# Two layers of a gated mixture-of-experts kernel: the second layer's shared weights are loaded and split earlier, and its shared blocks follow their tile by two steps instead of three

## The chip, the cores and the metric

The kernel runs on one core of one Trainium2 chip. The metric is the device time of one execution in microseconds. Three runs of the kernel before took 1601.77, 1603.18 and 1605.84 us, median 1603.18.

## The reference

The input x has 4 x 512 tokens of 512 numbers. Two layers are added to it one after the other. Each layer first mixes over the tokens (a decaying sum forward and backward along the tokens, over a side input, divided by the same sum of weights, times a sigmoid of x), and then applies a mixture of experts. Layer 0 has an RMS norm, 8 experts of inner size 256 of which each token takes 2, and one shared expert. Layer 1 has 32 experts of inner size 352 of which each token takes 6, and two shared ones, which are run as two halves.

```python
# layer 1, cut to what matters
top_w, top_i = lax.top_k(softmax(xf @ gate_w.T), 6)
routed = sum over the 6 of  top_w * ((silu(x @ w1[e]) * (x @ w3[e])) @ w2[e])
shared = silu(xf @ sw1) * (xf @ sw3) @ sw2
x = x + routed + shared
```

## The kernel before

The tokens are 16 tiles of 128. The work is a sequence of blocks of 128 tokens. Block 0 to 15 are layer 0's shared expert, 16 to 54 its routed blocks (39), 55 to 86 layer 1's shared blocks (32, two for each tile, one for each half of the shared weights), and 87 to 214 its routed blocks (128). For each block TensorE multiplies by gate and up (`gu_pe`, line 1714), ScalarE takes a tanh and VectorE finishes H (`gu`), TensorE transposes H (`h_turn`, 1752), ScalarE and VectorE split it into a high and a low half in float16, TensorE multiplies by the down weights (`down`, 1778), and ScalarE (line 1222) or VectorE (line 1594) takes the result out.

Weights are products of three float16 matmuls, so each weight is needed as a high and a low half. `pieces` (line 80) cuts them into pieces of 1024 or 1088 columns. A piece is loaded by SyncE (`w_load`, 918) into one of two staging buffers ST, whose order is RING, or, for the pieces in AHEAD, straight into a part of Whi or Wlo that is not yet used. ScalarE then makes the high half (`w_hi`, 1148: one pass where VectorE makes the low half, two passes where POOL does), and VectorE (`w_lo`, 1542) or POOL (`w_lo`, 971) the low half. A ring load waits until the piece two before it in the ring has its low half. Pieces 0 to 26 are layer 0's, 27 to 34 layer 1's shared weights (27 to 30 for even shared blocks, 31 to 34 for odd ones), 35 and up layer 1's experts. In `pieces` 27, 29, 31 and 33 belong to VectorE and 28, 30, 32 and 34 to POOL, and 35 to 50 to POOL. `spare` (731) gives the block after whose `down` the place of a piece may be written: for 27 to 50 that is block 54, the last routed block of layer 0.

The order of all work is written out by hand in `stages` (115), a generator. Every engine walks it and takes what is its own, so the order in it is the program order of each engine. After layer 0's shared blocks a loop over j runs from 0 to 41 (line 392). Step j has `gu_pe` of block 16+j, a half of a unit of the second layer's scan in two of three steps, `h_turn`, `gu`, `h_low`, and `down` of block 13+j. A unit of the scan has 128 channels of one batch: the first half is two forward scans, a scaling on ScalarE (1073, 1075) and two backward scans (1285 to 1299), and the second half is sums and a reciprocal (1306 to 1321), with two products on POOL (955, 963). Then TensorE turns the result (`k_turn`) and ScalarE writes it to RT (1092). At j from 37 to 40 SyncE issues `y_load`, the first of which waits for the last RT. For the routed blocks POOL gathers rows (`gather`, 978) into three buffers XG and SyncE transposes them by DMA (`x_turn`, 894) into four buffers XSp.

Then come `pick` 0 and 1 (POOL gathers the routed results of layer 0), four pieces by `weights`, and `x_sum` 0 and `f_tanh` of the first tile. `x_sum` (1335) adds what was picked into the tile. A loop over s from 0 to 17 (line 429) follows. Step s has, for tile s: the turn of tile s-1 on TensorE (`f_turn`, 1630), `gate` of tile s on VectorE (1324), `f_hi` on ScalarE (1116) and `f_lo` on VectorE (1353), both in the one buffer XG[2], `row` and `x_turn` on SyncE. `f_hi` waits for the transposition of the tile before. Then come two slots h, each with one shared block b = 2(s-3)+h: `gu_pe` of b, `h_turn` of b-1, `gu` of b, `down` of b-2. In between stand the logit of the tile before, `x_sum` and `f_tanh` of the next, and after every fourth tile the routing: `r_top`, `r_red`, then `r_pos`, `r_wts`, `r_slot`. `hot` makes two 0/1 matrices on VectorE, `hot_pe` multiplies them; there are 24 of each, and from the third on `hot` waits until the `hot_pe` two before is done. The step ends with two pieces of weights (one from s=4 on). After the loop come hot 18 to 23, the last blocks, hot_pe 18 to 23 and the gathers for block 87. `hot_pe` 18 stands behind `gu_pe` of block 86.

Of the kernel before, what the change touches and what calls it, by code (L numbers as in the profile page):

```python
# [92 lines left out]

AHEAD = (17, 18, 19, 20)
RING = [k for k in range(len(PIECES)) if k not in AHEAD]


# [15 lines left out]
def stages():  # L115
# [24 lines left out]
    def weights(n, upto):  # L140
        for _ in range(n):
            yield from loads(2, upto)
            yield from splits(1)
            yield from loads(2, upto)
# [247 lines left out]
    for j in range(NB0 + 3):  # L392
        n = R0 + j
        if n + 3 < S1:
            yield "gather", n + 3
        if n + 2 < S1:
            yield "x_turn", n + 2
        if n < S1:
            yield "gu_pe", n
        yield from turn_made()  # L400
        if j * 27 // 39 != (j - 1) * 27 // 39 or j >= 39:
            yield from next_half()
        if n - 1 < S1:
            yield "h_turn", n - 1
        if n < S1:
            yield "gu", n
        yield from after_half()
        if n - 2 < S1:
            yield "h_low", n - 2
        if 1 <= j:  # L410
            yield "down", n - 3
        if 37 <= j < 41:
            yield "y_load", j - 37
    while half[0] < 64:
        yield from next_half()
        yield from after_half()
    yield from turn_made()
    for i in range(2):
        yield "pick", i
    yield from weights(4, 51)  # L420
    yield "x_sum", 0
    yield "f_tanh", NT

    def shared(b, what):

        if 0 <= b < 32:
            yield what, S1 + b

    for s in range(18):
# [11 lines left out]
        if s < 8:  # L441
            yield "k_back", s + 8
        for h in (0, 1):
            b = 2 * (s - 3) + h
            slot = 2 * s + h
            yield from shared(b, "gu_pe")
            yield from shared(b - 1, "h_turn")
            yield from shared(b, "gu")
# [97 lines left out]
def build(nc, xtok, fT, cst, svec, cond, rout, gatew, W0, W1, Y1):  # L546
    with ExitStack() as ctx:
# [5 lines left out]
        def sem(name):  # L553
            return ctx.enter_context(nc.semaphore(name))
# [104 lines left out]
        d_pick = [sem(f"d_pick{i}") for i in range(2)]  # L659
        d_first = sem("d_first")  # L660
        d_w = [sem(f"d_w{i}") for i in range(2)]
        d_ahead = sem("d_ahead")
        d_g = [sem(f"d_g{i}") for i in range(3)]
        d_t = [sem(f"d_t{i}") for i in range(4)]
        d_row = [sem(f"d_row{i}") for i in range(6)]
# [55 lines left out]
        def staged(k):  # L721

            l, e, c0, cw, at, who = PIECES[k]
            if k in AHEAD:
                m = AHEAD.index(k)
                to = 18432 + 3072 * (m // 2)
                return (Whi, Wlo)[m % 2][:, to:to + 2 * cw].bitcast(F32), d_ahead, 16 * (m + 1)
            m = RING.index(k)
            return ST[m % 2][:, 0:cw], d_w[m % 2], 16 * (m // 2 + 1)

        def spare(k):

            if k < 27:
                return None
            m = (k - 27) // 4
            if m < SLOTS1:
                return S1 - 1
            return R1 - 1 if m - SLOTS1 < 2 else R1 + 4 * (m - SLOTS1 - 2) + 3
# [96 lines left out]
        def _(eng):  # L835
# [82 lines left out]
            def w_load(k):  # L918
                l, e, c0, cw, at, who = PIECES[k]
                if k not in AHEAD and k >= 2:  # L920
                    eng.wait_ge(*low(RING[RING.index(k) - 2]))
                at, there, count = staged(k)
                S.dma_start(at, WD[l][e][:, c0:c0 + cw]).then_inc(there, 16)

# [121 lines left out]
        def _(eng):  # L1046
# [101 lines left out]
            def w_hi_(k):  # L1148
# [3 lines left out]
                eng.wait_ge(there, count)  # L1152
                if k == 21:

                    for j in AHEAD[-2:]:
                        eng.wait_ge(*low(j))
                if spare(k) is not None:
                    eng.wait_ge(b_down, spare(k) + 1)
# [73 lines left out]
        def _(eng):  # L1232
# [230 lines left out]
            def hots(h):  # L1463

                A16, B16 = AB[h % 2][:, 0], AB[h % 2][:, 1]
                if h >= 2:
                    eng.wait_ge(r_tab, 1 + h - 1)
                else:
                    eng.wait_ge(b_down, S1)
                n0 = 4 * h % 24  # L1470
                V.tensor_tensor(A16, bc(iota16[:, :].unsqueeze(1), [P, 4, P]),
                                bc(qa[:, n0:n0 + 4].unsqueeze(2), [P, 4, P]), ALU.is_equal)
# [393 lines left out]
```

## Time and profile before

| | us |
|---|---|
| median of 3 runs | 1603.18 |
| the profiled execution | 1601.73 |
| its span, first to last instruction | 1599.6 |
| TensorE (PE) busy in the span | 1342.6 (84%) |
| VectorE (DVE) busy | 1006.1 (63%) |
| ScalarE (ACT) busy | 742.2 (46%) |
| GpSimd (POOL) busy | 604.6 (38%) |

The shares are means over very different stages: layer 0 until some 513 us, the shared stage of layer 1 until some 807 us, then its routed blocks. Times in the rows are microseconds from the start of the span. An entry in brackets is the time that the engine was idle before the instruction, and what released it.

### The profile page before, as it was taken

Reading aid. Unit: us, or ns where it says so; the run is one execution under the profiler, and the core shown is the slowest. Engines: PE = TensorE matmul, PEld = TensorE weight load, DVE = VectorE, ACT = ScalarE, POOL = GpSimd, SP = SyncE. Lnnn points to the kernel's source line nnn. Section 1 sums busy time; section 2 is a strip of 40 time slices with the busy share of each in tenths; the row PEclk is TensorE's granted clock in tenths of the full one; section 3 lists DMA queues with packets and bytes.
Section 4 is the critical chain, followed back from the end, with each engine's and each line's share of the span. In section 5 each row is a group of like instructions: output and inputs, shape, how many; then the busy total and the mean of one; then the engine's idle time right before and its main releaser. Section 6 shows DMA issues by size and latency. Waiting matters only on the chain.

```text
span 1599.6 us, 23683 instructions
## 1 busy us (share of the span) xinstructions
PE 1342.6 (84%) x8220; PEld 811.3 (51%) x8220; DVE 1006.1 (63%) x1748; ACT 742.2 (46%) x1262; POOL 604.6 (38%) x466
## 2 busy tenths in 40 slices
PE   0146666699997289889899999999999999999998
PEld 0023342244443156556565666666666666666664
DVE  8999978979896468888735444444444444444222
ACT  4466664545454543333146454454444445444332
POOL 2344432544431443231033443444444444444443
PEclk9987766899999599999999999999999999999999
DMA  3557644689985896563048988889998988988664
GB/s 101 174 174 187 156 112 92 151 182 195 206 177 159 227 205 145 141 146 83 25 137 233 203 199 212 196 207 199 207 208 195 206 203 204 200 206 184 109 115 74
DMA packets 225234, 269.38 MB, mean 168 GB/s; under 512 B 149664, under 2 KB 149792, under 8 KB 224992
## 3 DMA queue, kind: packets, MB, share of 16 engines
q1 hardware_dynamic: 188464, 175.84, 42.6%
q0 software_dynamic: 36656, 92.03, 29.2%
q8 instruction: 70, 1.15, 0.3%
q14 instruction: 44, 0.36, 0.1%
HBM read 167.87 MB, written 70.32 MB: 149 GB/s over the span
## 4 chain that ended last, share of the span: by engine, by line
PE 60%; DVE 26%; issue 5%; DMA 4%; ACT 3%; POOL 1%; SPq 0%; POOLq 0%; ACTq 0%; DVEq 0%
PE psG L1749 33%; PE psO L1798 19%; DVE wkFD L1314 5%; PE psH L1766 3%; DMA ST<-W 2%; DVE wkFN L1289 2%; DVE wkFD L1296 2%; PE psX L1710 2%; DVE wkFD L1285 2%; DMA XSp<-XG 2%; DVE wkFN L1321 1%; DVE wkFD L1306 1%; DVE H L1574 1%; DVE Wlo L1555 1%; DVE wkFN L1299 1%
## 5 line engine op out<-in xcount | busy, mean ns | idle before, releaser
L1749 PE MATMUL psG<-Whi,XSp 128*128 128x352 f16 (+2 forms) x3000 | 671.8, 329 | 12.1 <-issue 10.8
L1749 PEld LDWEIGHTS psG<-Whi,XSp 128*128 128x128 f16 x3000 | 295.7, 100 | 212.5 <-issue 38.4
L1798 PE MATMUL psO<-Whi,HS 128*128 128x512 f16 (+1 forms) x1180 | 394.5, 387 | 0.0
L1749 PE MATMUL psG<-Wlo,XSp 128*128 128x352 f16 (+2 forms) x1500 | 389.2, 329 | 0.0
L1021 POOL DMA_INDIRECT out<-OB,posb x128 | 202.7, 1583 | 416.1 <-ACT OB L1222 407.5
L1555 DVE SCALAR_TENSOR_TENSOR Wlo<-ST,Whi 128x1088 f16<-128x1088 f32 (+1 forms) x118 | 152.3, 1291 | 235.4 <-ACT Whi L1168 231.4
L1574 DVE SCALAR_TENSOR_TENSOR H<-H,psG 128x352 f32<-128x352 f32 (+1 forms) x215 | 105.5, 491 | 242.2 <-ACT H L1187 221.4
L1798 PE MATMUL psO<-Wlo,HS 128*128 128x512 f16 (+1 forms) x590 | 228.4, 387 | 0.0
L1187 ACT ACTIVATE H<-psG 128x352 f32<-128x352 f32 (+1 forms) x215 | 95.2, 443 | 229.7 <-PE psG L1749 222.5
L1749 PEld LDWEIGHTS psG<-Wlo,XSp 128*128 128x128 f16 x1500 | 149.1, 99 | 93.4 <-issue 8.3
L1798 PEld LDWEIGHTS psO<-Whi,HS 128*128 128x128 f16 x1180 | 117.6, 100 | 120.4 <-issue 9.8
L1222 ACT ACTIVATE OB<-psO,WSL 128x512 f32<-128x512 f32 x128 | 88.1, 688 | 173.7 <-PE psO L1798 173.7
L1003 POOL DMA_INDIRECT XG<-xrows,posb x128 | 129.5, 1012 | 90.9 <-DVE posb L1486 42.4
L1168 ACT ACTIVATE Whi<-ST 128x1088 f16<-128x1088 f32 (+1 forms) x118 | 129.7, 1100 | 28.1 <-DMA ST<-W 28.1
L975 POOL TENSOR_TENSOR Wlo<-ST,Whi 128x1088 f16<-128x1088 f32 (+1 forms) x37 | 82.0, 2218 | 154.6 <-ACT Whi L1172 154.5
L1576 DVE SCALAR_TENSOR_TENSOR H<-H,psG 128x352 f32<-128x352 f32 (+1 forms) x215 | 106.4, 495 | 7.4
L1200 ACT CAST HS<-psH 128x384 f16<-128x384 f32 x160 | 75.7, 473 | 71.9 <-PE psH L1766 71.9
L963 POOL TENSOR_TENSOR wkFN<-wkFN,wkEU 128x512 f32<-128x512 f32 x32 | 40.5, 1267 | 180.6 <-DVE wkEK L1276 169.5
L1314 DVE RECIPROCAL wkFD<-wkFD 128x512 f32<-128x512 f32 x32 | 107.1, 3346 | 0.0
L1620 PE MATMUL psX<-C,wkFN 128*128 128x128 f32 x64 | 16.7, 412 | 101.9 <-DVE wkFN L1321 101.9
L1584 DVE TENSOR_TENSOR HS<-psH,HS 128x384 f16<-128x384 f32 x160 | 88.1, 551 | 16.2 <-ACT HS L1200 16.2
L1766 PE MATMUL psH<-C,H 128*128 128x128 f32 x480 | 80.5, 277 | 19.3 <-DVE H L1576 19.3
(216 smaller groups left out, 1536.9 us busy)
## 6 DMA issues: line engine op xcount, KB each, us to landing
ST<-W SPq DMA_DIRECT2D x136, 544.0 KB
ST<-W SPq DMA_DIRECT2D x23, 512.0 KB
slots<-OB SPq DMA_DIRECT2D x39, 256.0 KB
wkK<-fT SPq DMA_DIRECT2D x32, 256.0 KB
xrows<-XG SPq DMA_DIRECT2D x20, 256.0 KB, 4.4
y0rows<-x SPq DMA_DIRECT2D x8, 512.0 KB, 5.5
y0rows<-OB POOLq DMA_DIRECT2D x16, 256.0 KB, 4.3
out<-OB SPq DMA_DIRECT2D x16, 256.0 KB
```

Of the source, the lines that this page charges most:

```text
L1003: G.indirect_dma_start(out=XG[g % 3][:, 0:w], out_offset=None, in_=X[l][:, :], in_offset=bass.IndirectOffsetOnAxis(ap=idx[l][:, j:j + 1], ...
L1021: G.indirect_dma_start(out=Y1[:, :], out_offset=bass.IndirectOffsetOnAxis(ap=idx[1][:, j:j + 1], axis=0), in_=OB[o % 4][:, :], in_offset=N ...
L1168: op = A.activation(st if who == "pool" else hi, st, ACT.Copy, scale=WS)
L1187: A.activation(H32[a][:, 0:F], psG[a][0][:, 0:F], ACT.Tanh, scale=0.5 * UN).then_inc(b_tanh, 1)
L1222: A.activation(OB[o % 4][:, :], psO[bank(o)][:, :], ACT.Copy, scale=scale).then_inc(b_outa, 1)
L1314: V.reciprocal(FD[n % 2][:, :], FD[n % 2][:, :]).then_inc(k_rec, 1)
L1555: op = V.scalar_tensor_tensor(out=Wlo[:, at:at + cw], in0=st, scalar=WS, in1=Whi[:, at:at + cw], op0=ALU.mult, op1=ALU.subtract)
L1574: V.scalar_tensor_tensor(out=H, in0=H, scalar=1.0, in1=g, op0=ALU.add, op1=ALU.mult).then_inc(b_sil, 1)
L1576: V.scalar_tensor_tensor(out=H, in0=H, scalar=(-0.5, 0.5)[l] * XS * UN * UN, in1=u, op0=ALU.mult, op1=ALU.mult).then_inc(b_h, 1)
L1749: op = M.matmul(o, hx[:, x, q * P:q * P + P], w(half_, off + c, nn), start=first, stop=last)
L1766: op = M.transpose(bank_[:, q * P:q * P + P], H32[a][:, q * P:q * P + P], ident)
L1798: op = M.matmul(psO[bank(o)][:, :], hs(n)[:, x, q * P:q * P + P], columns[n](half_, off0 + q * 512, 512), start=(q == 0 and x == 0 and hal ...
```

## The change

AHEAD gets pieces 32 and 33, which are loaded into the place of layer 0's shared weights once all its shared blocks are done. Loads and splits of layer 1's shared weights are put into the loop over j, and the four pieces that stood before `x_sum` 0 are taken out. As the counters of `stages` work out, the loads are 27 and 28 at j=1, 32 at j=2, 33 at j=3, 29 and 30 at j=22, and 31 and 34 at j=37; the splits are 27 at j=20, 28 at j=21, 29 at j=35, 30 at j=36 and 31 at j=39. Step s=0 then splits 32 and 33, s=1 34 and 35, and so on, and the last pieces of the loop, 50, at s=14. `spare` lets 27 and 28 be written after block 31 (expert 0 has at most 16 blocks) and 29 to 31 after block 47. Two more waits guard the places of 32 and 33 before piece 47 and before `hot` 0 and 1. In the loop over s the shared block of slot 2s+h is now slot - 4, up to block 27 (of 0 to 31); steps 16 and 17 have one block each, 28 and 29, in their second slot.

```diff
-AHEAD = (17, 18, 19, 20)
+AHEAD = (17, 18, 19, 20, 32, 33)
...
         if 37 <= j < 41:
             yield "y_load", j - 37
+        if j in (1, 22, 23, 37):
+            yield from loads(2, 51)
+        if j in (2, 3):
+            yield "w_load", 30 + j
+        if j in (20, 21, 35, 36, 39):
+            yield from splits(1)
...
     for i in range(2):
         yield "pick", i
-    yield from weights(4, 51)
     yield "x_sum", 0
     yield "f_tanh", NT
...
         for h in (0, 1):
-            b = 2 * (s - 3) + h
             slot = 2 * s + h
+            b = slot - 4 if slot < 32 else {33: 28, 35: 29}.get(slot, -9)
...
-        d_ahead = sem("d_ahead")
+        d_ahead = [sem(f"d_ahead{i}") for i in range(6)]
...
             m = (k - 27) // 4
+            if k < 32:
+
+                return R0 + 15 if k < 29 else R0 + 31
...
+                if k in AHEAD and l == 1:
+
+                    eng.wait_ge(b_down, R0)
                 at, there, count = staged(k)
...
                 if k == 21:
 
-                    for j in AHEAD[-2:]:
+                    for j in AHEAD[2:4]:
+                        eng.wait_ge(*low(j))
+                if k == 27 + 4 * 5:
+                    for j in AHEAD[4:]:
                         eng.wait_ge(*low(j))
...
                     eng.wait_ge(b_down, S1)
+
+                    for j in AHEAD[4:]:
+                        eng.wait_ge(*low(j))
```

## Rows read from the trace of the kernel before

**Rows 1.** Windows: start:end, length, busy (instructions) by engine, TensorE clock, DMA share, GB/s.
```profile
core 0: us, PE busy (x) PEld busy (x) DVE busy (x) ACT busy (x) POOL busy (x), PEclk, DMA share, GB/s
340.00:360.00 20.00, 19.01 (x97) 9.46 (x95) 16.77 (x21) 11.16 (x26) 7.29 (x6) 1.00 1.04 237
...
550.00:560.00 10.00, 6.68 (x26) 4.67 (x27) 2.90 (x5) 4.25 (x6) 4.55 (x4) 0.50 1.17 256
...
662.55:724.09 61.54, 55.50 (x375) 36.14 (x375) 50.01 (x111) 21.79 (x37) 18.15 (x12) 0.97 0.57 141
...
752.57:788.10 35.53, 35.53 (x251) 22.97 (x249) 26.59 (x74) 5.21 (x13) 2.25 (x1) 1.00 0.07 25
```
**Rows 2.** Timeline of VectorE, 417 to 425 us: start, duration, instruction.
```profile
418.00 0.68 DVE L1306 SCALAR_TENSOR_TENSOR wkFD<-wkEU,wkFD 128x512 f32<-128x512 f32 x1
...
423.12 0.69 DVE L1321 SCALAR_TENSOR_TENSOR wkFN<-wkFD,wkFN 128x512 f32<-128x512 f32 x1
...
424.51 1.22 DVE L1285 TENSOR_TENSOR_SCAN wkFD<-dec,wkEK 128x512 f32<-128x512 f32 x1
```
**Rows 3.** Timelines of VectorE and ScalarE, 493 to 500 us.
```profile
494.25 0.42 DVE L1574 SCALAR_TENSOR_TENSOR H<-H,psG 128x256 f32<-128x256 f32 x1 [1.23 <-ACT H L1187]
...
495.04 1.22 DVE L1285 TENSOR_TENSOR_SCAN wkFD<-dec,wkEK 128x512 f32<-128x512 f32 x1
...
497.29 1.25 DVE L1296 TENSOR_TENSOR_SCAN wkFD<-dec,wkFD 128x511 f32<-128x511 f32 x1
...
494.96 0.60 ACT L1222 ACTIVATE OB<-psO 128x512 f32<-128x512 f32 x1 [0.47 <-PE psO L1798]
```
**Rows 4.** Timelines of SyncE's queue and of ScalarE, 504 to 524 us.
```profile
507.34 0.32 SPq L886 DMA_DIRECT2D wkK<-y0rows  x1
...
513.92 0.98 SPq L923 DMA_DIRECT2D ST<-W  x2
...
510.71 0.38 ACT L1205 ACTIVATE HS<-psH 128x256 f16<-128x256 f32 x1
...
512.93 0.60 ACT L1222 ACTIVATE OB<-psO 128x512 f32<-128x512 f32 x1 [0.70 <-PE psO L1798]
519.50 1.11 ACT L1168 ACTIVATE Whi<-ST 128x1088 f16<-128x1088 f32 x1 [5.97 <-DMA ST<-W]
```
**Rows 5.** Timelines of POOL, VectorE and TensorE, 505 to 560 us.
```profile
517.98 0.97 POOL L1035 DMA_INDIRECT wkFD<-slots,sl  x1 [14.76 <-DMA slots<-OB]
...
528.34 0.75 DVE L1341 SCALAR_TENSOR_TENSOR wkK<-wkFD,wk,wkK 128x512 f32<-128x512 f32 x1
...
531.87 2.30 DVE L1332 SCALAR_TENSOR_TENSOR XG<-XG,RT 128x512 f32<-128x512 f32 x1 [1.99 <-ACT XG L1108]
...
539.91 0.69 DVE L1332 SCALAR_TENSOR_TENSOR XG<-XG,RT 128x512 f32<-128x512 f32 x1
...
556.11 0.80 PE L1749 MATMUL psG<-Whi,XSp 128*128 128x352 f16 x2
```
**Rows 6.** The page's costliest groups: the splits of weights (busy, mean ns, idle before).
```profile
L1555 DVE SCALAR_TENSOR_TENSOR Wlo<-ST,Whi 128x1088 f16<-128x1088 f32 (+1 forms) x118 | 152.3, 1291 | 235.4 <-ACT Whi L1168 231.4
...
L1168 ACT ACTIVATE Whi<-ST 128x1088 f16<-128x1088 f32 (+1 forms) x118 | 129.7, 1100 | 28.1 <-DMA ST<-W 28.1
L975 POOL TENSOR_TENSOR Wlo<-ST,Whi 128x1088 f16<-128x1088 f32 (+1 forms) x37 | 82.0, 2218 | 154.6 <-ACT Whi L1172 154.5
```
**Rows 7.** Timeline of ScalarE, 417.5 to 424 us.
```profile
417.92 0.60 ACT L1222 ACTIVATE OB<-psO 128x512 f32<-128x512 f32 x1 [0.47 <-PE psO L1798]
```
**Rows 8.** Timelines of VectorE and POOL, 306 to 311 us.
```profile
307.33 3.08 DVE L1289 TENSOR_TENSOR_SCAN wkFN<-dec,wkEKV 128x512 f32<-128x512 f32 x1
...
306.71 2.62 POOL L975 TENSOR_TENSOR Wlo<-ST,Whi 128x1024 f16<-128x1024 f32 x1 [1.49 <-ACT Whi L1172]
```
**Rows 9.** Timelines of TensorE and VectorE, 752 to 792 us.
```profile
752.57 0.60 PE L1640 MATMUL psX<-C,XR 128*128 128x128 f32 x4
...
768.27 0.19 DVE L1384 MAX8 mx<-lg 128x8 f32<-128x32 f32 x1
...
788.10 0.69 DVE L1471 TENSOR_TENSOR Whi<-iota,qa 128x512 f16<-128x512 f16 x1 [1.44 <-PE psO L1685]
```

More of the change, by code:

```diff
@@ L726, in staged @@
                 to = 18432 + 3072 * (m // 2)
-                return (Whi, Wlo)[m % 2][:, to:to + 2 * cw].bitcast(F32), d_ahead, 16 * (m + 1)
+                return (Whi, Wlo)[m % 2][:, to:to + 2 * cw].bitcast(F32), d_ahead[m], 16
             m = RING.index(k)
```

## The prediction

> **What bounds the kernel now.** I read the windows by stage first, then the chain of waits, then the timelines of the engines where the change acts. While the first layer's routed blocks run, TensorE and VectorE are both nearly full, and the sixteen DMA engines are full in places: 19.0 and 16.8 of 20 us, DMA share 1.04 at 340 to 360 us [rows 1]. The reader should see there that this is no stage with room to spare. One unit of the scan (two halves on VectorE, with three blocks on TensorE) takes about 14.1 us: from 424.51 to 495.04 us five units pass [rows 2, 3]. VectorE waits in it for one loop (its H, the transposition, ScalarE's tanh), 1.23 us [rows 3], and for little else, so I read this stage as VectorE-bound: what VectorE loses there is not made up. In the second layer's shared stage four tiles take 61.5 us [rows 1], TensorE busy for 55.5 and VectorE for 50.0 of them. The shifting of blocks changes neither total, so I keep that cycle as it is. Between the stages TensorE does nothing useful from 512.9, when the last routed block's result is read [rows 4], to 556.11 us, when the first shared block starts [rows 5]. At the end of the shared stage TensorE is busy for all 35.5 us of 752.57 to 788.10 [rows 1].
>
> **The splits beside the routed blocks.** Five pieces (27 to 31) are loaded and split there, and 32 to 34 are loaded. A piece costs ScalarE 1.10 us, or two such passes if POOL makes the low half, and VectorE 1.29 us, or POOL 2.22 [rows 6]. Each engine takes them in program order, and what counts is who stands behind.
> Piece 27 (block j=20): its high half follows the scaling of `down` at 417.92 us on ScalarE [rows 7], so it runs from 418.5 to 419.6, and VectorE, which began its next half at 418.00, has to wait for it and then spends 1.29: 420.9. Cost 2.9 us on VectorE [rows 2, 6].
> Piece 28 (j=21) is POOL's. ScalarE's two passes for it end near 425.7, so its low half would start just as VectorE comes to k_out (423.12, shifted by 2.9, is 426.0) [rows 2]. When POOL subtracts, a VectorE operation with two inputs in SBUF waits: the scan at 307.33 took 3.08 us where one of the same size takes 1.22, and ended 1.1 after POOL did [rows 3, 8]. So k_out is pushed by about 1.8 us. Bounds: 0 (VectorE first) and 2.2.
> The Trainium skill, page SBUF — State Buffer, section on the shared port pair, says the same as a rule: whichever of the two starts first holds the pair for the whole instruction and the other fully blocks. By that rule piece 28 costs nothing if k_out comes a moment before POOL, and piece 30 costs the same; the sum would be 1.8 lower. The rows show the unlucky order, so I keep 1.8.
> Piece 29 (j=35) is VectorE's and falls into the idle 1.23 us before 494.25 [rows 3]: 0.1.
> Piece 30 (j=36): ScalarE finishes `down` at 495.56 and then makes two passes to 497.8, so its scaling of the forward scan comes late; the backward scan, at 497.29 before, would start at 498.5 [rows 3], meets POOL's subtraction and ends at about 501.3 instead of 498.5. Cost 2.8; bounds 1.2 (no meeting) and 3.
> Piece 31 (j=39): its load is issued behind the first y_load, which SyncE can issue only at 507.34, when the last RT is written [rows 4]. The first ring load of before was issued at 513.92 and its split started at 519.50 [rows 4], 5.6 later, so this one, issued after a store at about 507.7, is there at about 513.1. ScalarE waits for it and then takes 1.1, and the last block's low half, at 510.71 before, and its `down` stand behind. The last routed result then comes at 516.0 to 516.6 instead of 512.93. Cost 3.1; bounds 1 (the load lands in 4 us) and 5. The cover that looks plentiful, ScalarE's idle time, is gone here because ScalarE is made to wait for a DMA.
> Sum: 2.9 + 1.8 + 0.1 + 2.8 + 3.1 = +10.7 us at the end of the first layer.
> **The DMAs.** Eight loads of 544 KB are issued there, about 2.3 us of all DMA engines each at the 237 GB/s of 340 to 360 us [rows 1], four of them between 320 and 337 us, SyncE also waiting for all first-layer shared blocks before piece 32. Gather and transposition follow each other through three buffers, so late landings can stop TensorE; VectorE has some lead over them in two of three blocks. I take +1; bounds 0 and +7.
>
> **Between the layers.** The last `down` to the gate of the first tile: before, the result was read from 512.93, pick started at 517.98, x_sum at 528.34 (VectorE had two low halves to make), and the gate, blocked by a POOL subtraction for 1.6 us, ended at 531.87 + 2.30 = 534.17 [rows 4, 5]: 20.6 us after 513.5. After: nothing is loaded at the same time, so I put pick 3.1 after the result (before 4.4), its two issues and their landing at 5.8, then x_sum 1.5, tanh 0.6, gate 0.7: 11.8 us. Gain 8.8, with bounds 7 and 9.5. Then some is given back. Tile 1's gate ended at 540.60 [rows 5], 6.4 after tile 0's. Now pieces 32 (POOL) and 33 (VectorE) stand ahead of it: x_sum and both halves of tile 0 2.8, tanh 0.6, ScalarE 3.3, then a VectorE low half that waits for POOL's, 2.4, gate 0.7: 9.85. Loss 3.4. The next step holds two blocks at the low clock (clock 0.50 still at 550 to 560 us in the first blocks of before [rows 1]), and I put the first block about 1.7 us behind the turn of tile 1 and the turn of tile 2 at 15.0 us after the gate of tile 1. Before, the turn of tile 2 stood 14.6 after it, just ahead of the block at 556.11 [rows 5]: +0.4, and one step more +0.3. Net: -8.8 + 3.4 + 0.7 = -4.7. What is late next is again the tile chain: gate, high half, low half, transposition, one after the other in one buffer; starting the blocks a step earlier does not shorten it.
>
> **The end of the shared stage.** Two blocks are already done when the last tile is turned (752.57 [rows 9]), so steps 16 and 17 hold one each. Four steps hold eight blocks in 55.5 us of TensorE time [rows 1], some 6.2 each without the turns and logits. If TensorE bounded all of it, that were -12. But the last routing sum starts at 768.27, behind the logit and one block's `down` and hot matrices on VectorE [rows 9], and TensorE now reaches hot_pe 15 and 17 before VectorE has made them: it waits about 2.3 us twice. I get the routing sum 3.6 us earlier, r_pos, then no longer behind a block, 5.4 earlier, and hot 20, which waits for hot_pe 18 behind block 86 at 788.10 [rows 9], 5.5 earlier. After that all is as before. -5.5, bounds -3.5 and -7.5.
>
> **Sum.** +10.7 + 1 - 4.7 - 5.5 = +1.5 us on the profiled execution's 1601.7 (its span 1599.6 and 2.1 around it), which lies 1.5 below the median of the three runs, 1603.2. For the median that makes 1604.7; forecast 1604.5, no change that can be measured: a measurement of this kernel tells some 0.3% (4.8 us) from no change.
>
> **Rivals.** *The splits are hidden* (0.26). VectorE's delays are made up because TensorE, busy for 19.0 of 20 us [rows 1], takes its turn as the bound, and the load of piece 31 lands early; the layer end moves by 3 us, not 11. For it: VectorE is idle for 3.2 of 20 us, ScalarE for about nine [rows 1]. Against it: five units in a row average 14.1 us, and the 1.23 us of waiting is a fixed round trip, not TensorE being late. Time 1604.5 - 7.5 = 1597.
> *TensorE bounds everything* (0.04): the earlier start comes through, hardly anything is given back, about -15: 1589.
> *The loads starve the ring* (0.26), on the other side: four loads before 337 us and two at 428 us delay the gathers and with them the transpositions; in a stage at DMA share 1.04 the backlog of 9 us is worked off slowly, and each block that lands late holds VectorE's gate/up step. It decides as soon as a transposition lands over 2 us later than now. Price +7: 1611.5.
> *The change does not do what it says*: if `b_down` or the ring's counts held the early loads back, the splits would wait on ScalarE in the middle of the blocks. The counts work out (ring loads 27 and 28 need only pieces 25 and 26), so I leave it inside the starved case.
>
> **Numbers.** The forecast's own case has 0.44 and reaches from 1599 to 1609. A small part of the hidden and of the starved case also ends within 0.3%. The whole range goes to 1594 (the hidden case with the tail's better bound) and 1612 (the starved case). Left out are the TensorE case and the far ends, 0.15 or so. Faster 0.27, same 0.49, slower 0.24.
>
> **What would show it.** On the timeline of VectorE the unit with j=20 to 22 is longer by 4 to 5 us and that with j=36 by about 3; ScalarE shows a wait for a DMA before the last split of the first layer; the last routed result comes about 11 us later, at 524. The first x_sum follows it by 9 to 10 us, and the first shared block starts near 549, still at the low clock. Turn of tile 15 is about 7 us later than 752.6, the first routed block of the second layer about 1 later than 807. If the last routed result comes before 518, the first sum is wrong and the kernel is faster; if TensorE shows waits of over 2 us for XSp between 330 and 450 us, the starved case holds. If hot_pe 15 and 17 show no wait, the end gains more than I say.

## The result and the profile after

The changed kernel took 1609.6 us (median of 20 runs), the kernel before 1604.3 us (20 runs beside it). The ratio is 1.0033, with a 95% interval from 1.0018 to 1.0048: slower by about 5.3 us, a small difference that the interval just tells from no change. The forecast was 1604.5 us, no change; the time is inside its whole range (1594 to 1612), and just above the 1609 up to which its own case reaches. The profiled execution took 1609.4 us with a span of 1607.5, 7.9 us more than the span of the one before.

The page of the changed kernel, its head:

```profile
span 1607.5 us, 23686 instructions
...
PE 1346.7 (84%) x8220; PEld 809.3 (50%) x8220; DVE 1007.3 (63%) x1748; ACT 741.5 (46%) x1262; POOL 603.0 (38%) x466
```

No total says anything: the work is the same, moved. Windows of the changed kernel, columns as in [rows 1], the last two being the four steady tiles and the end of the shared stage:

```profile
440.00:450.00 10.00, 7.75 (x32) 3.75 (x31) 5.94 (x7) 2.99 (x7) 2.69 (x3) 0.83 0.94 214
...
674.70:736.29 61.59, 55.61 (x374) 36.15 (x374) 49.93 (x111) 21.79 (x37) 18.15 (x12) 0.97 0.61 140
764.90:793.08 28.18, 24.33 (x179) 15.63 (x177) 21.29 (x66) 3.43 (x8) 0.00 (x0) 1.00 0.07 22
```

The steady tiles are what they were (61.54 before). The end is 7.35 us shorter than the 35.53 of before, and TensorE is no longer busy all through it. In the window at 440 us, in which TensorE now idles for more than 2 us and part of the time has the low clock, lies one of the two large things that the forecast had put too low.

Since both kernels run the same instructions, every one can be paired with itself. The table is made so, from the start times of six of them: the first scan of units 25 and 31, ScalarE's read of the last routed result, the turns of tiles 5 and 15, and VectorE's first gate/up operation of block 87. The column before is in us, the others are the difference to it; one profiled execution each. The kernels e1 to e12 are told below.

| stage | before | changed | e1 | e2 | e3 | e4 | e6 | e7 | e9b | e10b | e11b | e12 |
|---|---|---|---|---|---|---|---|---|---|---|---|---|
| A: scan units 25 to 31 | 84.5 | +8.2 | +5.1 | +8.1 | +6.2 | +2.4 | +2.4 | +0.9 | +0.4 | +0.1 | +0.4 | 0.0 |
| B: to last routed result | 17.9 | +5.6 | +5.0 | +2.8 | +5.1 | -0.1 | -0.2 | -0.5 | -0.3 | 0.0 | -1.6 | -0.6 |
| C: to turn of tile 5 | 87.9 | -1.3 | -3.8 | -2.0 | -5.2 | +10.2 | -3.9 | -14.2 | -14.4 | -11.4 | -7.7 | -4.2 |
| D: to turn of tile 15 | 151.7 | +0.3 | +0.3 | +0.4 | +0.4 | -0.1 | +0.2 | 0.0 | +0.4 | +4.5 | +0.3 | +0.1 |
| E: to block 87 | 59.1 | -7.0 | -7.0 | -7.0 | +0.1 | -5.6 | -5.6 | 0.0 | +3.4 | 0.0 | -7.0 | -7.0 |
| A to E | 401.1 | +5.8 | -0.4 | +2.4 | +6.6 | +6.8 | -7.1 | -13.9 | -10.5 | -6.8 | -15.6 | -11.7 |

Behind E, where the code is the same, the profiled executions differ by up to 3 us from the one before (the changed kernel: +2.5). Ahead of A only the first four early loads are new. The twelve kernels that have them there, e5 and e8 included, reach A by -0.5 to +5.2 us later, 2.8 on average (the changed kernel: -0.5), and e4, which has not, 0.4 earlier. Within a stage two executions of the same code differ too: A of e4 is 2.4 longer than A of the kernel before, and A of e6 2.0 longer than A of e11b. So the table attributes, differences of some 2 us in it are not to be trusted singly, and the medians judge.

Stage A in the changed kernel. VectorE at the splits of pieces 27 and 28:

```profile
417.48 0.42 DVE L1594 SCALAR_TENSOR_TENSOR H<-H,psG 128x256 f32<-128x256 f32 x1
419.37 1.29 DVE L1573 SCALAR_TENSOR_TENSOR Wlo<-ST,Whi 128x1088 f16<-128x1088 f32 x1 [1.47 <-ACT Whi L1183]
420.57 0.68 DVE L1321 SCALAR_TENSOR_TENSOR wkFD<-wkEU,wkFD 128x512 f32<-128x512 f32 x1
...
425.69 2.47 DVE L1336 SCALAR_TENSOR_TENSOR wkFN<-wkFD,wkFN 128x512 f32<-128x512 f32 x1
```

The half that began at 418.00 in [rows 2] begins at 420.57: the wait of 1.47 for the high half and 1.29 of work, 2.8 us against the run's own offset of -0.2 there. Then k_out takes 2.47 instead of 0.69, 1.8 us, because POOL's subtraction had begun before it:

```profile
425.37 2.24 POOL L987 TENSOR_TENSOR Wlo<-ST,Whi 128x1088 f16<-128x1088 f32 x1 [0.37 <-ACT Whi L1187]
```

And then SyncE's queue:

```profile
434.78 0.93 SPq L935 DMA_DIRECT2D ST<-W  x2
435.80 1.23 SPq L916 DMA_TRANSPOSE XSp<-XG  x1
...
437.75 3.39 SPq L916 DMA_TRANSPOSE XSp<-XG  x1
```

and TensorE, for the block that waits for it:

```profile
442.87 0.39 PE L1767 MATMUL psG<-Whi,XSp 128*128 x1 [2.25 <-DMA XSp<-XG]
...
444.71 0.63 PE L1767 MATMUL psG<-Wlo,XSp 128*128 x1
445.14 1.06 PE L1767 MATMUL psG<-Whi,XSp 128*128 x2
```

The loads of pieces 29 and 30 go out together at 434.78. The transposition behind them takes 3.39 us to issue (1.30 at its place before) and lands so late that TensorE waits 2.25 us; after that its matmuls take 0.63 instead of 0.38 (clock 0.83 over the window above), and the scan's turn and both engines behind it stand 3.95 us later.

Stage B: VectorE at pieces 29 and 30.

```profile
500.68 1.28 DVE L1573 SCALAR_TENSOR_TENSOR Wlo<-ST,Whi 128x1088 f16<-128x1088 f32 x1
502.00 0.42 DVE L1592 SCALAR_TENSOR_TENSOR H<-H,psG 128x256 f32<-128x256 f32 x1
...
506.08 2.75 DVE L1311 TENSOR_TENSOR_SCAN wkFD<-dec,wkFD 128x511 f32<-128x511 f32 x1 [0.96 <-ACT wkFD L1085]
```

SyncE's queue at piece 31:

```profile
518.08 0.32 SPq L895 DMA_DIRECT2D wkK<-y0rows  x1
518.44 0.91 SPq L935 DMA_DIRECT2D ST<-W  x2
```

and ScalarE there, to the last routed result:

```profile
523.16 1.11 ACT L1183 ACTIVATE Whi<-ST 128x1088 f16<-128x1088 f32 x1 [2.62 <-DMA ST<-W]
...
526.24 0.60 ACT L1237 ACTIVATE OB<-psO 128x512 f32<-128x512 f32 x1 [1.21 <-PE psO L1816]
```

Piece 29 costs nothing: the gate/up operation behind it comes 7.75 us later than in [rows 3], as all around it. Piece 30 costs 2.5 (0.96 of waiting, and a scan of 2.75 instead of 1.25). Piece 31 costs 3.0: its load stands behind the first y_load, ScalarE waits 2.62 us for it, and the last result comes at 526.24.

Stage C, VectorE: the first sum, the gate of tile 0, the low half of piece 33 and the gate of tile 1.

```profile
535.89 0.75 DVE L1356 SCALAR_TENSOR_TENSOR wkK<-wkFD,wk,wkK 128x512 f32<-128x512 f32 x1 [10.29 <-DMA wkFN<-slots,sl]
...
538.12 0.69 DVE L1347 SCALAR_TENSOR_TENSOR XG<-XG,RT 128x512 f32<-128x512 f32 x1 [0.69 <-ACT XG L1120]
...
545.49 2.43 DVE L1573 SCALAR_TENSOR_TENSOR Wlo<-Wlo,Whi 128x1088 f16<-128x1088 f32 x1 [3.84 <-ACT Whi L1183]
547.84 0.68 DVE L1347 SCALAR_TENSOR_TENSOR XG<-XG,RT 128x512 f32<-128x512 f32 x1
```

The sum is 9.65 us behind the last result (15.41 before), the gate of tile 0 ends 12.6 behind it (21.2 before), and the gate of tile 1 comes 9.7 behind that.

### The profile page after: what moved, and what is told of

The parts are those of the page before. It is cut to its first block, busy times and chain, and to the rows that moved or that the text cites. A ratio compares the mean times of both kernels' runs of the same rounds, so it can differ in the third digit from the quotient of the medians.

```text
span 1607.5 us, 23686 instructions
## 1 busy us (share of the span) xinstructions
PE 1346.7 (84%) x8220; PEld 809.3 (50%) x8220; DVE 1007.3 (63%) x1748; ACT 741.5 (46%) x1262; POOL 603.0 (38%) x466
## 4 chain that ended last, share of the span: by engine, by line
PE 36%; DVE 26%; issue 16%; DMA 9%; POOL 7%; ACT 4%; POOLq 0%; SPq 0%; ACTq 0%; DVEq 0%
PE psG L1767 19%; PE psO L1816 12%; DVE wkFD L1329 5%; POOL out L1033 4%; DMA out<-OB,posb 4%; POOL XG L1015 3%; DMA ST<-W 3%; DVE wkFN L1304 2%; DVE wkFD L1311 2%; PE psH L1784 2%; DVE wkFD L1300 2%; DVE wkFN L1336 1%; DVE wkFD L1321 1%; DVE H L1592 1%; PE psX L1728 1%
## 5 line engine op out<-in xcount | busy, mean ns | idle before, releaser
L1602 DVE TENSOR_TENSOR HS<-psH,HS 128x384 f16<-128x384 f32 x160 | 88.0, 550 | 15.2 <-ACT HS L1215 15.2
```

## The experiments

Three questions were open: what the early splits and loads cost and why, whether the shift of the shared blocks is a gain, and whether places exist at which the same work costs nothing.

**e1: the two loads apart.**

```diff
-        if j in (1, 22, 23, 37):
+        if j in (1, 37):
             yield from loads(2, 51)
+        if j in (24, 28):
+            yield from loads(1, 51)
```

> The loads of pieces 29 and 30 are issued one by one, at j=24 and j=28, instead of together at j=22; all splits stay where the change puts them. In the changed kernel TensorE waits 2.25 us for XSp at 442.87 us and then runs a few us at the low clock, 4.0 us in all. Theory A (the two loads, 1.1 MB, stand ahead of a transposition on the DMA engines): the wait is gone, the scan unit that starts at 453.11 before is again 3.8 us late, not 7.8, and the last routed result of the first layer comes at 522.3 instead of 526.24 us. Theory B (POOL's low half of piece 28 holds back two gathers by 5 us, and those are what comes late): the wait stays, last routed result at 525.5 or later. Time about 1605.5 by A, 1609.5 by B.

One run: 1602.58 us. In the window in which the changed kernel has 7.75 us of TensorE work at clock 0.83:

```profile
440.00:450.00 10.00, 10.00 (x53) 5.06 (x51) 9.86 (x11) 5.33 (x12) 4.43 (x4) 1.00 1.05 206
```

Unit 27 takes 14.05 us instead of 18.01; theory A. POOL's low half of piece 28 and the gathers behind it are unchanged, so they are not the cause. e2 and e5, which keep the pair of loads, have the wait again (2.21 and 2.00 us) and a unit 27 of 18.0 and 17.6 us. e3 keeps it too and waits 2.29 us, but has no low clock there: its unit 27 takes 16.4. So some 2.3 of the 3.95 us are the wait and 1.6 the clock. A single load is no guarantee either: in this run TensorE waits 1.38 us for XSp at 453.88, which costs nothing, and in e8, also with single loads, 3.08 us at 455.66. The last routed result came at 523.97 and not at the expected 522.3, because this run was 2.3 us behind already at unit 26, 1.5 of it from ahead of the stage. The rest of the 7 us is not shown to come from the loads: stage C is 2.5 us shorter too, told below, and behind block 87 this run had 2.1 less.

**e2: the load of piece 31 ahead of y_load.** The four lines of the loads at j in (1, 22, 23, 37) and of y_load change places.

> The loads of j (31 and 34 at j=37) stand ahead of y_load instead of behind it; nothing else is moved. Theory A (ScalarE waits 2.6 us for a load that is issued only at 518.4 us, behind a y_load that waits for the last RT): the load is issued near 508 us, ScalarE's wait for it is gone, the last routed result comes 3.0 us earlier, at 523.2 instead of 526.24 us, and the time is about 3 us shorter, 1606.5. Theory B (the last down is late for another reason, TensorE's low clock or the chain of the last scan unit): under 1 us earlier, 525.3 or later, time unchanged.

One run: 1606.87 us. SyncE's queue and then ScalarE, at the same place as above:

```profile
510.18 0.93 SPq L935 DMA_DIRECT2D ST<-W  x2
519.91 0.33 SPq L895 DMA_DIRECT2D wkK<-y0rows  x1
```

```profile
521.82 0.60 ACT L1237 ACTIVATE OB<-psO 128x512 f32<-128x512 f32 x1 [1.39 <-PE psO L1816]
522.31 1.10 ACT L1183 ACTIVATE Whi<-ST 128x1088 f16<-128x1088 f32 x1
```

The high half follows the result before it without a wait, and stage B is 2.7 us shorter (expected 3.0; the last result itself is at 525.33, the run being 1.8 us behind already at unit 26). Theory A.

**e3: the changed kernel without the shift.**

```diff
-            b = slot - 4 if slot < 32 else {33: 28, 35: 29}.get(slot, -9)
+            b = slot - 6
```

> The changed kernel with the shared blocks three steps behind their tile again (slot - 6), the rest as changed. Theory A (the shift moves two blocks of TensorE time from the end of the shared stage into the steps of the first tiles, where they are paid as well: 7.3 us later there, 7.0 earlier at the end): the turn of tile 15 comes near 757.5 us instead of 764.9, the first routed block of the second layer stays within 1.5 us of the changed kernel's, time 1609.5, ratio to before 1.003. Theory B (the steps of tiles 1 to 4 are long because the high halves of pieces 34 and 35 stand ahead of f_hi on ScalarE, not because of the blocks): the turn of tile 15 stays near 763, the gain at the end is lost, time 1615, ratio 1.007.

1611.3 us (8 runs), ratio 1.0038 (1.0016 to 1.0060). Neither theory as put: stage C is 3.9 us shorter than in the changed kernel and stage E 7.1 longer. By the stages the shift gains about 3 us here; the ratios to the kernel before, 1.0038 and 1.0033, cannot tell it from nothing.

**e4: the kernel before with only the shift.** The opposite line, in the kernel before.

> The kernel before with only the shift of the shared blocks (slot - 4); loads and splits as before. Theory A (the shift is paid in the steps of the first tiles with what it gains at the end): the turn of tile 15 comes about 7 us later than 752.57 us, near 759.5, the first routed block of the second layer within 1.5 us of 807.4, time 1604, ratio 1.000 with 0.002 either way. Theory B (the shift is a gain by itself): the turn of tile 15 within 2 us of 752.6, the first routed block 5 to 7 us earlier, time 1598, ratio 0.996.

1609.7 us (12 runs), ratio 1.0036 (1.0019 to 1.0053): the shift alone makes the kernel before slower, which neither theory had. Stage C costs 10.2 us and stage E gives back 5.6. (Stage A is 2.4 longer there although its code is that of before: VectorE waits 2.7 us for ScalarE's scaling instead of 0.5; why stays open.) So by stages C to E the same edit is worth -3 in one kernel and +4.5 in another. TensorE's low clock explains little of that: half of TensorE's busy time in the low stretches of stage C, an estimate of what they cost, is 9.0 us in e4 and 7.7 in the kernel before, 8.2 in the changed kernel and 9.3 in e3. What differs is how much the two blocks lengthen the steps that they fall into. The gates of tiles 2 to 4 (VectorE), in e4:

```profile
551.29 0.68 DVE L1332 SCALAR_TENSOR_TENSOR XR<-XR,RT 128x512 f32<-128x512 f32 x1
...
565.97 0.69 DVE L1332 SCALAR_TENSOR_TENSOR XR<-XR,RT 128x512 f32<-128x512 f32 x1 [0.69 <-ACT XR L1108]
...
582.85 0.69 DVE L1332 SCALAR_TENSOR_TENSOR XR<-XR,RT 128x512 f32<-128x512 f32 x1 [0.69 <-ACT XR L1108]
```

and in e3:

```profile
552.55 0.69 DVE L1347 SCALAR_TENSOR_TENSOR XR<-XR,RT 128x512 f32<-128x512 f32 x1 [0.70 <-ACT XR L1120]
...
561.97 0.69 DVE L1347 SCALAR_TENSOR_TENSOR XR<-XR,RT 128x512 f32<-128x512 f32 x1 [0.69 <-ACT XR L1120]
...
577.29 0.69 DVE L1347 SCALAR_TENSOR_TENSOR XR<-XR,RT 128x512 f32<-128x512 f32 x1 [0.70 <-ACT XR L1120]
```

From the gate of tile 2 to that of tile 3 it is 14.7 us with two blocks in the step and 9.4 without (9.15 in the kernel before); from there to that of tile 4 it is 16.9 and 15.3 (13.4 before).

**e5: pieces 32 and 33 split ahead of the first sum.** 32's low half is VectorE's, `splits(2)` stands ahead of `x_sum` 0, and steps 0 and 1 split none and one.

> The changed kernel with the splits of pieces 32 and 33 moved ahead of the first x_sum, where ScalarE and VectorE wait 9.65 us for the picked rows; 32's low half is VectorE's; step 0 splits nothing, step 1 only piece 34. Theory A (those two splits, 3.3 us, stand between the gates of tiles 0 and 1, and nothing else uses the wait for the pick): x_sum 0 still 9.7 us after the last routed result, the gate of tile 1 is 6.4 us behind that of tile 0 instead of 9.72, and with one piece less ahead of f_hi 2 the turn of tile 5 comes 3 to 5 us earlier; time about 1605. Theory B (the tile chain is set by picks and by the one buffer, the splits lie beside it): the gate of tile 2 keeps its distance of 14.0 us to that of tile 0, time unchanged at 1609.

One run: 1610.8 us. The gate of tile 1 comes 4.2 us behind that of tile 0 (expected 6.4, 9.7 in the changed kernel), but that of tile 2 takes 9.5 instead of 4.3, so of 5.5 us 0.3 are left there: for these two gates theory B. With one high half less ahead of f_hi the next step is 2.7 us shorter, and stage C as a whole 4.5 (-5.8 against -1.3), as theory A has it. Stage D is 4.5 longer, and so the time did not fall. That is TensorE's low clock. From the turn of tile 5 to that of tile 6, first in this run, then in the changed kernel:

```profile
611.98:628.77 16.79, 15.21 (x88) 9.23 (x89) 13.18 (x29) 5.42 (x9) 4.66 (x3) 0.90 0.50 147
612.88:628.04 15.16, 13.58 (x89) 8.72 (x90) 13.18 (x29) 5.42 (x9) 4.66 (x3) 1.00 0.57 157
```

VectorE, ScalarE and POOL do the same work in the same time; TensorE has idled for 1.35 us at the same place in both, and in e5 a low stretch of 3.4 us follows. It is so again in two later steps (clock 0.84 and 0.90 where the changed kernel has 0.91 and 1.00); by the estimate above the low stretches cost 4.6 us more in this stage D. Why they appear in this run is not shown. Without them it would have come near the 1605 of theory A.

**e8: only the places of 27 and 28.** Loads as in e1, and

```diff
-        if j in (20, 21, 35, 36, 39):
+        if j in (22, 26, 35, 36, 39):
             yield from splits(1)
```

> The changed kernel with single loads at j=24 and 28 and only the splits of pieces 27 and 28 moved, to j=22 and j=26; 28's low half is still POOL's. Theory A (what costs is that VectorE must wait for a high half, or that POOL's subtraction meets a two-input operation of VectorE): 27 costs under 0.3 us at j=22 (2.8 at j=20); 28 costs 1.1 to 2.3 us, since POOL's 2.2 us meet VectorE's scans wherever they lie. Theory B (any split in this stage costs VectorE its own length): 27 costs 1.3 us, 28 nothing.

One run: 1607.3 us. Its k_out on VectorE:

```profile
455.72 2.50 DVE L1338 SCALAR_TENSOR_TENSOR wkFN<-wkFD,wkFN 128x512 f32<-128x512 f32 x1
```

beside POOL's low half of piece 28:

```profile
455.43 2.25 POOL L989 TENSOR_TENSOR Wlo<-ST,Whi 128x1088 f16<-128x1088 f32 x1 [0.41 <-ACT Whi L1189]
```

and the same piece at the same place on VectorE, in e7 (told below):

```profile
454.91 0.42 DVE L1600 SCALAR_TENSOR_TENSOR H<-H,psG 128x256 f32<-128x256 f32 x1
455.25 1.28 DVE L1579 SCALAR_TENSOR_TENSOR Wlo<-ST,Whi 128x1088 f16<-128x1088 f32 x1
456.56 0.42 DVE L1598 SCALAR_TENSOR_TENSOR H<-H,psG 128x256 f32<-128x256 f32 x1
```

Unit 27 is 15.95 us long in e8 and 13.98 in e7. The low half "for nothing" on POOL costs VectorE 1.8 us in k_out (2.50 instead of 0.69), and the one on VectorE itself costs 0.0, because it fills the 1.23 us that VectorE waits for the tanh. That all of the unit's 1.9 us is POOL's doing e8 does not show alone, since TensorE is late in it too:

```profile
455.66 0.39 PE L1769 MATMUL psG<-Whi,XSp 128*128 x1 [3.08 <-DMA XSp<-XG]
```

It ends this block at 458.27 and k_out ends at 458.22, and the turn of the unit needs both. In the changed kernel the lock stands by itself: there TensorE idles 2.37 us until k_out is done. Piece 27 at j=22 was not free as expected: VectorE waits 0.82 us for its high half (in e7), and unit 26 takes 15.1 to 15.9 us in the four runs that have it there. At j=26 (e9b and e12) it is free: units 26 and 27 take 14.1 and 14.0 us in e9b, 14.6 and 14.0 in e12, and 14.5 and 14.1 in the kernel before.

**e6 and e7: everything moved, with and without the shift.** All low halves of the shared weights on VectorE and, in the loop and behind it:

```diff
+        if j == 36:
+            yield from loads(1, 51)
         if 37 <= j < 41:
...
-        if j in (1, 22, 23, 37):
+        if j == 1:
...
-        if j in (20, 21, 35, 36, 39):
+        if j in (22, 26, 35):
+            yield from splits(1)
+        if j in (24, 28):
+            yield from loads(1, 51)
...
         yield "pick", i
+    yield from splits(4)
     yield "x_sum", 0
+    yield from loads(2, 51)
...
-        yield from weights(2 if s < 4 else 1, 51)
+        yield from weights((0, 1, 2, 2)[s] if s < 4 else 1, 51)
```

e7 has `b = slot - 6` besides.

> The changed kernel with every split where the traces show an engine waiting: 27, 28 and 29 at j=22, 26 and 35 (ahead of VectorE's 1.23 us waits), 30 to 33 ahead of the first x_sum, all low halves of the shared weights on VectorE, loads one by one at j=24, 28 and 36, piece 34 in step 1. Theory A (each cost of the change is one of place): the scan units keep 14.0 us, the last routed result comes 17.9 us after the start of the last unit as before (23.45 in the changed kernel), gate of tile 1 some 10 us earlier than before, 3 to 4 us given back in steps 2 to 4, 7 gained at the end of the shared stage: 13 us less than before, time 1590, ratio 0.992. Theory B (VectorE has no room for a low half beside a routed block: each of the 1.23 us waits is a round trip that the high half on ScalarE lengthens): each of the three splits costs 1.1 to 1.3 us and the time is about 1595.

> As e6_all_moved, but with the shared blocks three steps behind their tile. It prices the shift in the better kernel. By the two stage tables so far (shift costs 3.9 in the steps of tiles 3 and 4 and gains 7.1 behind tile 15 in the changed kernel; 9.0 and 5.6 in the kernel before): theory A, the shift gains 3 us, time 3 us above that of e6; theory B, it gains nothing, as in the kernel before, since the steps of the first tiles are shorter and the blocks stand in the way of the tile chain: time as e6 or up to 3 us below.

e6: 1600.1 us (12 runs), ratio 0.9958 (0.9940 to 0.9976). e7: 1593.2 us (6 runs), ratio 0.9922 (0.9896 to 0.9948). Stages A and B are down to +0.9 and -0.5 in e7, so the cost of the early splits was one of place, as theory A of e6 has it. e6 missed the 1590 us of that theory all the same, since stage C gives back more than the 3 to 4 us expected and stage E gains 5.6 and not 7. Of e7, theory B holds, and by more than its 3 us: the shift is a loss of 6.9 us by the medians and of 4.9 by stages C to E: C 10.3 longer, D 0.2, E 5.6 shorter. Of the 10.3, 2.4 are TensorE's low clock, by the same estimate (7.8 us in stage C of e6, 5.4 in e7), and whether the shift brings them is not shown. VectorE's gates of tiles 2 to 4, in e6:

```profile
544.84 0.68 DVE L1353 SCALAR_TENSOR_TENSOR XR<-XR,RT 128x512 f32<-128x512 f32 x1
...
555.80 0.69 DVE L1353 SCALAR_TENSOR_TENSOR XR<-XR,RT 128x512 f32<-128x512 f32 x1 [0.70 <-ACT XR L1126]
...
570.66 0.69 DVE L1353 SCALAR_TENSOR_TENSOR XR<-XR,RT 128x512 f32<-128x512 f32 x1 [0.69 <-ACT XR L1126]
```

and in e7:

```profile
543.78 0.68 DVE L1353 SCALAR_TENSOR_TENSOR XR<-XR,RT 128x512 f32<-128x512 f32 x1
...
548.09 0.69 DVE L1353 SCALAR_TENSOR_TENSOR XR<-XR,RT 128x512 f32<-128x512 f32 x1 [0.70 <-ACT XR L1126]
...
561.20 0.69 DVE L1353 SCALAR_TENSOR_TENSOR XR<-XR,RT 128x512 f32<-128x512 f32 x1 [0.70 <-ACT XR L1126]
```

The step from tile 2 to 3 is 11.0 us with the blocks and 4.3 without. The faster the first tiles can go, the more the blocks in their steps cost.

**e9b: from e7, the places once more.** 27 and 28 at j=26 and 32, the loads of 29 and 30 at j=28 and 34, those of 34 and 35 behind the picks, one split in each of steps 1 to 17.

> From e7_all_moved_no_shift (three steps behind): piece 27 at j=26 and 28 at j=32 instead of j=22 and 26, loads 29 and 30 at j=28 and 34, the loads of 34 and 35 only in step 0, behind the picks, and one split in each of the steps 1 to 17 instead of two in steps 2 and 3. Theory A (each place by its own row): 27 now costs nothing (0.8 at j=22), x_sum 0 comes 9.7 us behind the last routed result instead of 11.3, the gates of tiles 3 to 5 come about 4 us earlier with one high half instead of two ahead of f_hi: 5 us less than e7, 1588, ratio 0.989. Theory B (the two splits now in steps 16 and 17 meet the routing and the hot matrices, where POOL's low half blocks VectorE and ScalarE's passes delay the copies): 2 to 4 us are lost behind tile 15, time as e7, ratio 0.992.

1595.3 us (6 runs), ratio 0.9944 (0.9927 to 0.9961). Theory B: stage E is 3.4 us longer. POOL's low half at 760.47 stands beside the last routing, and hot 20 comes 21.5 us behind the routing sum instead of 19.8. Piece 27 is free and x_sum 0 is at 10.1 us, but the gates of tiles 3 and 4 did not move, and that of tile 2 comes 10.0 us behind that of tile 1 instead of 9.4.

**e10b: nothing split beside the routed blocks.** 27 and 28 loaded early and split ahead of x_sum 0, two pieces in each of steps 0 to 5, no shift.

> Nothing is split beside the routed blocks: 27 and 28 are loaded early and split ahead of the first x_sum, 29 to 34 in steps 0 to 2, 35 and up two per step to step 5; shared blocks three steps behind. Theory A (what the change gains lies between the layers, not in the early splits): the routed stage and its last result as before, x_sum 0 10 to 11.3 us behind it instead of 15.4, gates 1 and 2 as in the kernel before, so 5 to 6 us less than before: 1599, ratio 0.9965. Theory B (the four splits more in the steps cost what they cost elsewhere): the gates of tiles 3 to 6 are 2 us later each and the time is as before, ratio 1.000.

1603.4 us (12 runs), ratio 0.9986 (0.9969 to 1.0004). Both theories hold in part: stages A and B are those of before, C is 11.4 shorter, and 4.5 of it is lost in stage D, where steps 4 and 5 now hold two splits. The loss is in one step, from the turn of tile 5 to that of tile 6 (19.8 us instead of 15.2): beside POOL's second low half an operation of VectorE takes 2.17 us instead of 0.18, then TensorE idles for 3.55 us instead of 1.35 and has the low clock for 6.8 us, so that it is busy 2.7 us longer. The table has -6.8, the medians -1.4; the profiled execution, 1597.2 us, was the quickest of its 12. So against e7 with its early splits this is the weaker kernel, by 10 us in the medians; early splits at free places are worth having.

**e11b: e6 with the last split in step 14.** `(0, 2, 2, 2)[s]` for `(0, 1, 2, 2)[s]`.

> e6_all_moved with two splits in step 1 instead of one, so that the last split (piece 50) falls in step 14 and not 15. Theory A (the gain behind tile 15 is 7.0 us in the changed kernel and 5.6 in e6 because POOL's low half of piece 50 blocks VectorE's hot matrices ahead of the last routing sum): the routing sum comes 10.3 us behind the turn of tile 15 instead of 13.25. Theory B (it is the clock or another stage): it stays at 13.2. The steps of tiles 2 and 3 together 1 to 2 us longer. Time 1597 to 1600.

One run: 1590.4 us. The hot matrix and the routing sum behind the turn of tile 15 (754.50 in e6, 747.41 in e11b), VectorE of e6:

```profile
755.31 2.25 DVE L1495 TENSOR_TENSOR Wlo<-iota,qa 128x512 f16<-128x512 f16 x1
...
767.75 0.18 DVE L1405 MAX8 mx<-lg 128x8 f32<-128x32 f32 x1
```

and of e11b:

```profile
748.22 0.68 DVE L1495 TENSOR_TENSOR Wlo<-iota,qa 128x512 f16<-128x512 f16 x1
...
757.75 0.18 DVE L1405 MAX8 mx<-lg 128x8 f32<-128x32 f32 x1
```

13.25 us in e6 and 10.34 in e11b. Theory A: with the split of piece 50 in step 15, POOL's subtraction (at 754.77 in e6) holds the hot matrix for 2.25 us, and the routing sum comes 2.9 us later. Half of that reaches block 87: stage E gains 7.0 in e11b and 5.6 in e6. The time, 7 us below the expected 1597, is mostly not this edit's doing. Stages A and B, with the same code as in e6, were 3.4 us shorter in this run, and of the 3.8 us in stage C, where 1 to 2 us more were expected, 3.1 are TensorE's low clock by the same estimate. The changed kernel, whose last split is in step 14 thanks to the early ones, has this gain; the kernel before with the shift (e4) has not.

**e12: e11b with the free places of e9b.**

> The changed kernel's shift of two steps kept, with the last split in step 14 (as e11b_last_split_out), and the early splits at j=26, 32 and 35, which cost VectorE nothing in e9b_tuned, with loads 29 and 30 at j=28 and 34. Theory A (the shift costs what TensorE's time of two blocks costs in steps 2 to 4 and gains 7 behind tile 15 once the last split is out of the way, so that it is a gain of its own): from the start of the last scan unit to the first routed block of the second layer 16 us less than before, time 1590, ratio 0.991, level with or 1 to 2 us better than e7_all_moved_no_shift. Theory B (what the single look at e11b showed was luck with TensorE's low-clock stretches, and the shift loses as it did between e6 and e7): time 1597 or more, ratio 0.995.

1595.6 us (6 runs), ratio 0.9935 (0.9914 to 0.9957). Between the theories, nearer to B: against e7 the shift costs 10.0 in stage C (2.3 of it the low clock, by the same estimate) and gains 7.0 in stage E. Of the difference in stage C between e12 and e11b, 3.5 us, 1.7 is one stretch at TensorE's low clock in the step of tile 5, which e11b did not have. e7 has the best median of all, and its interval overlaps with that of e12: whether the shift costs or gains anything at its best is not settled.

## Why the prediction was right or wrong

The time lies in the whole range, and the change of 0.33% just beyond the 0.3% that the forecast called no change. That is in part luck: 1609.6 is nearer to the 1611.5 of the starved rival than to the 1604.5 forecast, and two steps that came out some 3 us dearer than forecast each were partly made up by an end 1.5 us better and by splits 0.6 cheaper. The turn of tile 15 came 12.3 us later (forecast 7), and block 87's first gate/up operation on VectorE 5.3 later (1 forecast for the block). By the forecast's own steps, with +5.8 us measured for stages A to E where they gave +1.5:

- **Pieces 27 to 31**, forecast 2.9, 1.8, 0.1, 2.8 and 3.1, in sum 10.7. Measured 2.8, 1.8, 0.0, 2.5 and 3.0, in sum 10.1, less 0.5 that the kernel before loses in unit 26 and the changed one does not. The method holds: each price came from who stands behind the split on its engine. e1, e2, e8 and e7 confirm the reasons: the wait for the load, POOL's lock, the idle 1.23 us. On the lock, the row is POOL at 425.37 and k_out at 425.69, held to 428.1. The Trainium skill (SBUF — State Buffer, the section on two separate sides) says that the one that starts first holds the shared ports for its whole instruction; the trace agrees, and in e8 again. The case that would have cost nothing, VectorE first, came nowhere: ScalarE's second pass ends while the reciprocal runs, and k_out always comes after.
- **The DMAs**, forecast +1, bounds 0 to +7. This is the first step that failed. Measured 3.95 in unit 27, shown by e1 to come from the pair of loads at j=22, and of which 1.6 is TensorE's low clock after its wait. Beside it, units 17 to 20, over which the first four loads go out, take 67.5 us on average in the twelve kernels that have them there (67.1 in the changed one) and 66.2 and 65.0 in the two that have not. It shows most in unit 20: 14.8 and 14.9 us without the loads, 15.7 (the changed kernel) to 18.6 with them. That they cause it is argued from this comparison; no run moves them alone. By the sign that the forecast itself named, a wait of over 2 us for XSp between 330 and 450 us, it is the case of the starved ring that held, though at one place and at about half its price. I had spread a backlog over the whole stage and looked at the loads one by one; at that place it mattered how much went out in one piece just ahead of a transposition.
- **Between the layers**, forecast -4.7, measured -1.3. Its first terms hold: -8.7 to the gate of tile 0 (-8.8), +3.3 to that of tile 1 (+3.4), the turn of tile 2 14.7 us behind the end of that gate (15.0; 14.6 before). What failed is "one step more +0.3". Behind the turn of tile 2 the changed kernel loses another 4 us to the turn of tile 5. About 1.5 of it is put down to the blocks, which fill these steps earlier, and 2.5 to two stretches at TensorE's low clock that fall on full steps: e1, with the same order there, has neither stretch, loses 1.6 between these turns and has a stage C of -3.8. One of them, in `down`, where the matmuls otherwise take 0.38:

```profile
589.61 0.55 PE L1784 MATMUL psH<-C,H 128*128 128x128 f32 x3 [1.70 <-DVE H L1594]
...
591.20 0.63 PE L1816 MATMUL psO<-Wlo,HS 128*128 128x512 f16 x1
591.62 1.06 PE L1816 MATMUL psO<-Whi,HS 128*128 128x512 f16 x2
```

- **The end of the shared stage**, forecast -5.5 (-3.5 to -7.5), measured -7.0. The routing sum came 5.4 earlier (3.6), hot 20 another 2.0, and 0.3 was given back. hot_pe 15 and 17 did wait, 1.84 and 0.76 us instead of 2.3 each. What I had not seen is that the last split falls in step 14 now: 2.9 at the routing sum and 1.4 of stage E (e6 against e11b), which is all of the miss.
- **The parts together.** That I took the shift as "the totals do not change, so the cycle stays" was right for the steady tiles and wrong as a way to price the edit. It does not remove work; it moves two blocks, some 12 us of TensorE time, from a place where TensorE is the bound to one where it may or may not be. In the kernel before and in e7 that place was not free.

Of the rivals, the hidden splits and TensorE as the bound did not hold.

## What to carry to other kernels

A piece of work put "beside" other work is paid at the engine that stands behind it: look for the one place in the cycle where that engine already waits, and put it on that engine (0.0 us at j=26 and 35) rather than on the idle POOL, whose subtraction holds VectorE back (1.8 us). Look at what large loads do to the small transfer behind them that a matmul is waiting for: two issued together ahead of it cost 3.95 us here, though issued singly they can still delay one (e8). An order that takes work off a full end pays only as much as it does not add to a chain at the start; by the stages the same line was -3, +5 and +5 us in three versions of one kernel, so price it again after every other edit.

## What the runs showed that was not expected

TensorE's low clock is worth a few us here and moves with unrelated edits. In full steps a stretch at 1.2 GHz follows now and then where TensorE has idled, but the idle time alone does not decide: after the same 1.7 us there is one in the changed kernel (clock 0.83 over 585 to 595 us) and none in e1 and e5, and after the same 1.35 us one in e5 and none in the changed kernel. The step from the gate of tile 4 to that of tile 5 takes 21.2 us in seven of the profiled kernels and 22.9 in six others, with nearly the same instructions in it, according to whether such a stretch falls on it. A wait of 2.25 us for a transposition cost 3.95 in this way. In e5 such stretches hid the 4.5 us gained in stage C, so a single run of a variant says little by its total.
